# Gathering the last slots of two tile pairs of a graph network layer in one DMA each

## What is computed

```python
# layer 0, for each node: its first 25 neighbours, their features' maximum
agg = feats.max(axis=2)                       # 0 joins the maximum when degree <= 25
x1 = layernorm(x + relu(concat([x, agg]) @ W + b))
# layer 1: attention of a node over its neighbours, 8 heads of 32
Wh = x1 @ W1;  s1 = Wh . a1;  s2 = Wh . a2
e = leaky(s1[i] + s2[j] + edge_emb[adj])      # -1e9 where adj is 0
h = softmax(e) @ Wh
out = layernorm(x1 + elu(layernorm(h) * gamma + beta))
```

## Time and profile before

| | |
|---|---|
| median of 3 runs | 3497.86 us (3492.01 to 3498.03) |
| the profiled execution | 3493.1 us, its span 3491.4 us |
| POOL busy | 2515.1 us (72%) |
| DVE busy | 2372.5 us (68%) |
| PE busy | 1589.2 us (46%) |
| ACT busy | 1115.7 us (32%) |
| PE's granted clock, mean | 0.69 of full speed |

### The profile page before, as it was taken

One profiled execution on the slowest core, in us unless ns is written; L12 is line 12 of the kernel. 1 busy time (PEld: TensorE's weight loads), 2 busy tenths in 40 slices (PEclk: granted clock), 3 DMA queues, 4 the chain that ended last, 5 costly groups with the idle time before them and its releaser, 6 DMA issues.

```text
span 3491.4 us, 25323 instructions
## 1 busy us (share of the span) xinstructions
PE 1589.2 (46%) x5123; PEld 1182.6 (34%) x5131; DVE 2372.5 (68%) x5655; ACT 1115.7 (32%) x2307; POOL 2515.1 (72%) x2640
## 2 busy tenths in 40 slices
PE   0045456344453444544365344554444443655544
PEld 0033334233332333333243233433333332444433
DVE  8797787665677667777597665867665543755466
ACT  3223344333343323433344232332222211233134
POOL 2576777777777777777777776777777777777675
PEclk9976567666676666666676666766676666767776
DMA  6667777655576555765567555564434443444332
GB/s 229 220 200 255 263 251 231 208 182 178 165 238 194 183 178 187 256 202 187 164 221 252 186 187 156 175 194 150 147 109 123 116 115 106 120 117 114 96 107 75
DMA packets 220561, 614.24 MB, mean 176 GB/s; under 512 B 66801, under 2 KB 110834, under 8 KB 193778
## 3 DMA queue, kind: packets, MB, share of 16 engines
q0 software_dynamic: 124416, 346.88, 33.4%
q1 hardware_dynamic: 95986, 265.69, 22.5%
HBM read 559.43 MB, written 52.95 MB: 175 GB/s over the span
## 4 chain that ended last, share of the span: by engine, by line
POOL 61%; issue 22%; DVE 8%; PE 4%; DMA 2%; DVEq 2%; ACT 1%; POOLq 0%; SPq 0%; ACTq 0%
POOL ring L549 53%; POOL sorted_d L527 4%; POOL out_dram L564 3%; DVE cand L970 2%; PE att_p L828 2%; DVEq L931 2%; DVE agg L1080 1%; DMA ring<-table_d,idx_loc 1%; POOL table_d L557 1%; DVE adj_h L966 1%; PE lin_p L792 1%; DVE ring L1234 1%; DVE agg L1073 0%; DMA ring<-sorted_d,idx_cur 0%; DMA ring<-in_x_dram,top_cur 0%
## 5 line engine op out<-in xcount | busy, mean ns | idle before, releaser
L549 POOL DMA_INDIRECT ring<-table_d,idx_loc x1128 | 1081.0, 958 | 396.3 <-issue 340.7
L549 POOL DMA_INDIRECT ring<-sorted_d,idx_cur x705 | 677.0, 960 | 214.9 <-issue 214.9
L800 PE MATMUL score_p<-ident,x1k 128*128 128x128 f32 x256 | 81.3, 419 | 1477.4 <-ACT x_t L638 1473.5
L1080 DVE TENSOR_REDUCE agg<-ring 128x256 f32<-128x2560 f32 (+9 forms) x120 | 453.1, 3776 | 344.4 <-DMA ring<-sorted_d,idx_cur 244.9
L828 PE MATMUL att_p<-ring,ident 128*128 128x256 f32 (+1 forms) x2384 | 607.9, 414 | 153.1 <-DVE ring L1234 153.1
L828 PEld LDWEIGHTS att_p<-ring,ident 128*128 128x128 f32 (+1 forms) x2384 | 500.0, 211 | 257.0 <-DVE ring L1234 158.5
L800 PEld LDWEIGHTS score_p<-ident,x1k 128*128 128x128 f32 x256 | 35.9, 197 | 1528.1 <-issue 1523.7
L669 ACT ACTIVATE neg<-z 128x256 f32<-128x256 f32 x128 | 53.3, 416 | 1430.1 <-DVE z L1123 1423.1
L549 POOL DMA_INDIRECT ring<-in_x_dram,idx_cur x423 | 404.0, 955 | 134.6 <-issue 128.0
L792 PE MATMUL lin_p<-w_s,h_t 128*128 128x256 f32 x1024 | 474.9, 644 | 0.0
L792 PEld LDWEIGHTS lin_p<-w_s,h_t 128*128 128x128 f32 x1024 | 320.9, 328 | 149.2 <-issue 81.0
(11 more groups left out here) (152 smaller groups left out, 2775.5 us busy)
## 6 DMA issues: line engine op xcount, KB each, us to landing
adj_i<-in_adj_dram SPq DMA_DIRECT2D x208, 1024.0 KB, 5.8
ring<-table_d,idx_loc POOLq DMA_INDIRECT x1128, 2.8
pay<-in_x_dram SPq DMA_DIRECT2D x8, 2048.0 KB, 10.0
xs<-sorted_d SPq DMA_DIRECT2D x128, 128.0 KB, 5.7
ring<-sorted_d,idx_cur POOLq DMA_INDIRECT x705, 2.9
table_d<-tab SPq DMA_DIRECT2D x80, 132.0 KB, 3.4
ring<-in_x_dram,idx_cur POOLq DMA_INDIRECT x423, 3.5
sorted_d<-pay,rank_i POOLq DMA_INDIRECT x128, 3.6
```

The lines of the kernel that those rows point to most:

```text
L549: pool.indirect_dma_start(out=to[:, k * width:(k + 1) * width], out_offset=None, in_=source, in_offset=bass.IndirectOffsetOnAxis(ap=idx_at ...
L1080: last = v.tensor_reduce(a, rows.rearrange("p (k c) -> p c k", c=C), AX, ALU.max)
```

## The change

Of the nodes in tiles 1, 2, 5 and 7 only the first 64 use the tile's last slot. The last slots of tiles 1 and 2 are now gathered by one DMA into a tile of their own, `pair_s`: the first 64 partitions for tile 1 and the last 64 for tile 2. The same is done for 5 and 7. Whichever tile of a pair comes first in its layer issues the pair's gather, after its other gathers; the other tile has one gather less. A graph has 141 gathers in each layer instead of 143.

- SP loads the pairs' row numbers, four more small DMAs for each graph (`pair_cur`), and DVE derives those of layer 1 (`pair_loc`).
- POOL waits for these words in layer 0 (`pair_ld`), and for the last use of `pair_s` by the pair before (`agg_ready` in layer 0, `logits_ready` in layer 1).
- `unpair` on DVE copies the 64 rows of a tile's half into its last slot, and fills the other 64 rows of that slot with a copy of the tile's first slot. It runs before the maximum in layer 0 and before the logits in layer 1, with a drain behind it.
- `slots_c`, the limits that a graph's degrees are compared with, takes one slot less for the rows from 64 up in the four tiles. Four more small fills stand at POOL's start.
- The ring has 55 positions instead of 56.

```diff
-RING = 56
+RING = 55
-CONSTS = 43
+CONSTS = 47
+PAIRS = [(1, 2), (5, 7)]
+HALF = P // 2
...
+def pair_of(layer, i):
+    u = (tile1(i) if layer else tile0(i))[1]
+    for c, pair in enumerate(PAIRS):
+        if u in pair:
+            there = [k for k in range(i - i % T, i) if (tile1(k) if layer else tile0(k))[1] in pair]
+            return c, pair.index(u), bool(there)
+    return None
+def gathers(layer, i):
+    pair = pair_of(layer, i)
+    return GATHERS[(tile1(i) if layer else tile0(i))[1]] - (1 if pair and pair[2] else 0)
+def pair_before(layer, i):
+    return max((k for k in range(i) if pair_of(layer, k) and pair_of(layer, k)[2]), default=None)
...
+                for c, pair in enumerate(PAIRS):
+                    for s, u in enumerate(pair):
+                        word = C + SLOTS[u] - 2
+                        sp.dma_start(pair_cur[g % 2][HALF * s:HALF * (s + 1), 2 * c:2 * c + 2],
+                                     sorted_d[g][u * P:u * P + HALF, word:word + 2].bitcast(I32)).then_inc(pair_ld, 16)
...
-                for k in range(GATHERS[u]):
+                pair = pair_of(layer, i)
+                for k in range(GATHERS[u] - (1 if pair else 0)):
                     pool.indirect_dma_start(
...
+                if pair and not pair[2]:
+                    c, used = pair[0], pair_before(layer, i)
+                    if layer == 0:
+                        pool.wait_ge(pair_ld, 16 * 2 * len(PAIRS) * (b + 1))
+                    if used is not None:
+                        pool.wait_ge(logits_ready if layer else agg_ready, used + 1)
+                    pool.indirect_dma_start(
+                        out=pair_s[layer][:, 0:width], out_offset=None, in_=source,
+                        in_offset=bass.IndirectOffsetOnAxis(
+                            ap=(pair_loc[b % 3] if layer else pair_cur[b % 2])[:, 2 * c + 1:2 * c + 2], axis=0),
                         bounds_check=None).then_inc(rows_ld[layer][i % 4], 16)
...
+            def unpair(layer, i, rows, width):
+                u, s = (tile1(i) if layer else tile0(i))[1], pair_of(layer, i)[1]
+                last = slice((SLOTS[u] - 1) * width, SLOTS[u] * width)
+                v.tensor_copy(rows[0:HALF, last], pair_s[layer][HALF * s:HALF * (s + 1), 0:width])
+                v.tensor_copy(rows[HALF:P, last], rows[HALF:P, 0:width])
...
+                    if pair_of(0, i):
+                        unpair(0, i, rows, C)
+                        settle()
...
+                    if pair_of(1, j):
+                        unpair(1, j, ring_tile(1, j), ROW)
+                        settle()
```

More of the change, by code:

```diff
@@ L126 @@
 RING_AT, RING_FREE = place_tiles()
+def pair_of(layer, i):
[8 more added lines that the diff above has]
+    return GATHERS[(tile1(i) if layer else tile0(i))[1]] - (1 if pair and pair[2] else 0)
 def gathered(layer, i):
-    return 16 * sum(GATHERS[(tile1(k) if layer else tile0(k))[1]]
-                    for k in range(i % 4, i + 1, 4))
+    return 16 * sum(gathers(layer, k) for k in range(i % 4, i + 1, 4))
+def pair_before(layer, i):
+    return max((k for k in range(i) if pair_of(layer, k) and pair_of(layer, k)[2]), default=None)
 def build(nc, x, adj, w0, b0, w1, a1, a2, emb, gamma, beta, out):
@@ L173, in build @@
         top_loc = [sb(f"top_loc{q}", [P, 2], I32) for q in range(3)]
+        pair_cur = [sb(f"pair_cur{q}", [P, 2 * len(PAIRS)], I32) for q in range(2)]
+        pair_loc = [sb(f"pair_loc{q}", [P, 2 * len(PAIRS)], I32) for q in range(3)]
+        pair_s = [sb(f"pair_s{layer}", [P, ROW]) for layer in range(2)]
         own_out = sb("own_out", [P, TILES], I32)
@@ L274, in build @@
         idx_ld = sem("idx_ld")
+        pair_ld = sem("pair_ld")
         rows_ld = [[sem(f"rows{layer}_ld{q}") for q in range(4)] for layer in range(2)]
@@ L497, in _ @@
             step(pool.memset(slots_c[0:TOPS, 0:1], float(SLOTS[0])))
+            for u in sum(PAIRS, ()):
+                step(pool.memset(slots_c[HALF:P, u:u + 1], float(SLOTS[u] - 1)))
             step(pool.memset(least_c[:, :], 0.5))
@@ L551, in gather @@
                         in_offset=bass.IndirectOffsetOnAxis(ap=idx_at(layer, b, u, k), axis=0),
+                        bounds_check=None).then_inc(rows_ld[layer][i % 4], 16)
+                if pair and not pair[2]:
[8 more added lines that the diff above has]
+                            ap=(pair_loc[b % 3] if layer else pair_cur[b % 2])[:, 2 * c + 1:2 * c + 2], axis=0),
                         bounds_check=None).then_inc(rows_ld[layer][i % 4], 16)
@@ L1047, in check_graph @@
                 v.tensor_scalar(top_loc[q][:, :], top_cur[b % 2][:, :], base, None, ALU.add)
+                dve.wait_ge(pair_ld, 16 * 2 * len(PAIRS) * (b + 1))
+                v.tensor_scalar(pair_loc[q][:, :], pair_cur[b % 2][:, :], base, None, ALU.add)
                 settle()
```

## The result

The changed kernel takes 3442.21 us in the median of four runs (3435.9 to 3443.46), the kernel before 3496.91 us beside it (3492.01 to 3498.03). The ratio is 0.984, with a 95% interval of 0.982 to 0.985, so some 55 us have gone. The forecast was 3440 us in a range of 3424 to 3474.

The account below looks back on a forecast made before the run. POOL was taken to bound the kernel. The terms -37.9 - 42.9 + 17.9 + 1 + 3 + 4 = -54.9 us gave 3438 us from the profiled execution, 3443 from the median; forecast 3440 us, range 3424 to 3474.

Parts of the forecast that it names:

- POOL sets the end: Whole kernel: POOL, though only 72% busy, determines when it ends; 61% of the last chain lies in its instructions.
- Gathers removed: POOL's queue: 32 gathers fewer at 1.263 us each, two absorbed by graph 0's table-tile waits, so 30 count: -37.9 us.
- The six waits: First gather of layer 1's wide tile in six graphs: POOL's waits for PE's sum vanish with the shorter ring, -42.9 us.
- Rival 1: POOL after the wide tiles: the removed waits return a few gathers later, at tiles such as 48; 3481 us, chance 0.10.
- The new wait at tile 112: Where the last two graphs meet: 27.6 us waiting for tile 111's sum, less 9.7 at 113 and 114: net +17.9 us.
- Tile 111: Layer 1, near the end: it now asks for tile 109 where it asked for 108, +1 us (0 to 3).
- Graph 0: Layer 0 of the first graph: four tiles' copies and deriving `pair_loc` on DVE delay table tiles, +3 us (2 to 4).
- The sign that I named: POOL's waits for table tiles in graph 0 would grow by 4 to 6 us in sum.
- Copies beside POOL: DVE's 128 unpairing copies stretch POOL's gathers running beside them: +4 us, between ends of 0 and 10 us.
- rival 2: DVE's unpairing copies: each blocks POOL for its whole length, 37 us in place of 4; 3471 us, chance 0.07.
- Rival 3: Tile 10 of layer 1 in six graphs: POOL waits for layer 0's wide maximum, slower; 3510 us, chance 0.05.
- Waits and loads added: Pairs' gathers, SP's four loads and POOL's four fills at its start: no wait paid and no delay, 0 us.

Follow-up runs that it names:

- the third group: Changed kernel, ring still 55, but six wide tiles of layer 1 wait again for PE's sum of the tile before: 4254.5 us, against 4155.1 us unmodified beside it.

## Why the prediction was right, point by point

The total came out 2 us from the median and 57.2 us against 54.9 in the profiled executions. Since the four executions of the changed kernel lie up to 7.6 us apart, an agreement this close is in part luck. The steps one by one:

- **POOL sets the end.** Right. That the sums over POOL's timeline come to 57.2 us says nothing, since such a sum does so for any engine. What bears it out is which lines hold the difference: the removed gathers and the waits named beforehand. Of DVE's 45.3 us of added work only the 3 us in graph 0 show. The page's chain of waits can't be read for it any more: it breaks off at the wait that is labelled "issue", and covers only 8% of the span (POOL 4%, issue 3%, DVE 1%).
- **Gathers removed, -37.9.** Right. Gathers and their steps give -39.4, with the stretch of the copies in it. The two in graph 0, layer 0, were absorbed by the waits for table tiles, as written.
- **The six waits, -42.9.** Right, and the term that carried most. All six have the bare step. Where I forecast 27 us of room at tile 15, there are 23. The experiments bear out the cause: the ring's length alone shortens them by 80 us while all 2288 gathers stay, down to what the whole change has in such a place (35.0 and 29.6 us for the six; the 80 us are against the pairs' kernel with its ring of 56), and six counts alone bring them back, at full price. Rival 1, that the waits come back in another place, failed: no wait stands at tiles 48 and 80, and the 1.48 us at tile 64 (the row at 1491.97) are all that can be put down to it. My reading that tile 48 has the least room was wrong, though. Before, from PE's sum to the first gather that asks for it, there are 4.35 us at tile 48, 2.86 at 64, 2.54 at 80, 1.78 at 96 and 3.77 at 112. Rival 1 was nearer than its 4.4 us made it.
- **The new wait at tile 112, +17.9 net.** Right: 28.1 us measured against 27.6, and 9.7 us gone at 113 and 114, +18.4 net. The same 27 to 30 us stand in every kernel with a ring of 55, but for those with tile 109 moved.
- **Tile 111, +1.** 0.55 us measured.
- **Graph 0, +3.** Right for what it priced. The waits for table tiles grew by 7.7 us, of which 2.5 us are the two absorbed gathers. That leaves 5.2 us. On DVE the four tiles with copies take 3.2 us, 0.8 us each where I put 0.7, and `pair_loc` 0.3 us where I put 0.2. The other 1.9 us come from the loads and belong to the last point below. The sign that I named, a growth of 4 to 6 us in sum, missed the 7.7.
- **Copies beside POOL, +4.** Mis-sized. The mean gather went from 0.9591 to 0.9598 us, over 2256 gathers 1.6 us, which is no more than two profiles of one program differ by. The 0.03 us a copy that the term took, and the 0.08 us read from one stretched gather, were too high as a mean: with 384 more copies it was 0.01 us each. Why most copies don't stretch a gather was not tested. By rival 2, each copy blocking POOL for its length, the mean gather would have been 0.975 us; the trace has 0.960, and the rival failed. The Trainium skill, "SBUF — State Buffer", section "Who interferes with whom", has a DVE instruction in a 2-port mode and GpSimd exclude each other for the whole instruction. Read as a price for each copy, that rule is not borne out by this trace.
- **Rival 3, POOL held by the wide maximum,** failed too: the maximum of tile 32 ends at 701.62 and is asked for at 719.63, 18 us apart as in the earlier trace rows.
- **Waits and loads added, 0.** Right for the waits: each of the 32 pairs' gathers has the bare step before it. Wrong for the loads, and this is the step of the prediction that failed. I asked only whether SP's four loads stand behind the ones that POOL's first gather needs. They also stand in front of the next loads of adjacency, which start 2.46 us later, and in graph 0 that goes through ACT's cast and DVE's search to the waits for table tiles: 1.9 us at the first maximum, where I had put 0.

The loads and the copies on DVE (+1.9 and +0.3) nearly cancel the lower price of the copies beside POOL (-2.4). The wait at tile 64 (+1.5), tile 112 (+0.5), tile 111 (-0.5) and some tenths in the gathers' steps come to less than 1 us. The 2.3 us between 54.9 and 57.2 then lie where no term spoke of anything: the scatters with their waits and the two ends of the span, -3.0 us in the table. So the near agreement of the totals rests in part on errors of 2 us that happen to cancel; the large terms were right each by itself.

The sum's own range of 3425 to 3458 us doesn't follow from the ends that the terms state: those give some 3429 to 3449 us. What widens it is not said. The measured time lies inside both.

## What to carry to other kernels

When a buffer that is used as a ring changes its length by one, write down for each user which earlier one it now waits for, before counting what the edit was made for: here that list was worth 43 us of gain and 18 us of loss, beside 38 us for the removed gathers. A wait that a long user had for its direct neighbour was paid in full here, 28 us at tile 112 and 84 us for the six in the third group. To ask for the neighbour before that was enough at the six wide tiles of the profiled result, but not where two wide tiles meet (16 us stayed with tile 109 moved). Such a gain can be tested from the other side, by putting the one count back into the changed kernel. And for loads that an edit adds, write down not only what they stand behind in their queue, but also what they stand in front of: here four small loads of 2.4 us held up the next load by as much, and 1.9 us of it reached DVE's chain in the first graph.

## What was not expected of the hardware

- The same program takes 3442 us in one place and 4155 us in another, with DVE busy for 2417.8 and 2413.5 us. The difference is idle time: up to 9 us at a time before the DVE instructions shown above, put down to nothing, and 36 us before one, put down to "remote". Its cause stays open.
- A wait of 28.43 us for a semaphore can stand in the profile as "issue". Where a wait is far over the usual step (0.30 us here), the name behind it is to be checked against the end of the work that the code waits for; here PE's row ended 0.75 us before.
- A copy of 64 x 256 in f32 takes 0.29 us and one added beside the gathers costs POOL 0.01 us by the difference of two profiles, some 0.02 us at most by their scatter, where a block for its length would be 0.29 us.
